# Eight staging buffers for values, key matrix products through six more banks, and eight token statistics ahead of the loop, in a fused cross-attention and expert layer

## The chip, the cores and the metric

The kernel runs on one core of one Trainium2 chip. The metric is device time in microseconds of one execution, the median of the runs taken; lower is better. TensorE (PE), VectorE (DVE), ScalarE (ACT), GpSimd (POOL) and SyncE (SP, which issues most of the DMAs) each work off a list of their own in order and wait for each other by semaphores.

## What is computed

`x` is 4 x 1024 x 256, the context 4 x 77 x 256. A cross-attention of 16 heads is added to `x`, then a layer of 9 experts, of which each token takes two:

```python
x = x + xattn(ctx, layernorm(x), fside)     # the tokens ask, the context answers
x = x + ffn(layernorm(x))

# xattn: kv = layernorm(ctx) @ Wkv; q = (layernorm(x) @ Wq) * (1 + scale) + shift
#        out = softmax(q k^T / 8) v, all heads, @ Wout
# ffn:   w, idx = top_k(softmax(x @ Wr), 2), w normalised to sum 1
#        out[t] = sum over the two experts of w * ((silu(x[t] @ Wg[e]) * (x[t] @ Wu[e])) @ Wd[e])
```

## The kernel before

All products are made in single-precision pieces: each operand is split into a rounded high part, which ScalarE writes, and the rest, which VectorE makes by subtraction; TensorE multiplies hi by hi, hi by lo and lo by hi.

The work has three stages. **Preparation** (to about 54 us) folds the weights into the context. A *key matrix* `keymat` holds Wq times the keys of each head, so that a token's scores are one product of its normalised row; a *value matrix* holds the values times Wout. **Attention** goes over 32 blocks of 128 tokens in steps: scores, softmax, product with the value matrix, routing, scatter of the rows to their experts. **Experts** goes over 40 tiles of rows (32 of 256 rows, 8 of 128) with weights that are loaded, split and multiplied.

The change touches the end of the preparation and the first two steps of attention.

*Key products.* The loop over `m` in 0 to 15 (`MATS`, PE from L1505) makes `keymat`: two matmuls for odd `m` (L1523), four for even `m` (L1523 and L1527), into a pair of PSUM banks that `mat_banks(m)` names. ScalarE copies the pair to `keymat_hi` (L1150, semaphore `mat_hi`), then VectorE subtracts to make `keymat_lo` (`mat_rest`, L1832, `mat_lo`); only then is the pair of banks free. Before the change the pairs are 4-5 and 6-7 in turn, with 2-3 for product 14, so that product `m` waits for the subtraction of product `m - 2`. Ahead of product 14 TensorE turns the first token block (`turn`, L1501, bank 5).

*Values.* Behind each of the first eight key products come two value products (`val`, L1489, two pairs of the banks 0 to 3), 16 in all. ScalarE (12 of them, L1133) and VectorE (4 of them, L1852) copy each to a staging buffer `val_st` in SBUF. Two products fill a buffer of four heads; SyncE stores a full one to DRAM in 4 or 6 DMAs (`store_vals`, L635), 8 buffers' worth in 40 DMAs. With `STORE_BUFFERS` of 4, filling 4 to 7 first waits for the store of the buffer four earlier (`val_stored`). Behind the 40, SyncE waits for them all to land (L641) and loads the value matrix back in the layout that attention wants (`load_valmat`, L651). The 8 late value products are made in the first two attention steps; VectorE copies them (L1852) into `late_f` and `valmat_f`, which lie over the memory of `val_st`, so each of those copies waits for all early stores: a wait on each of the `val_stored` semaphores (L1849).

*Token statistics.* VectorE takes batch statistics of the tokens (`token_stats`, L1838), two blocks behind each of the first seven key subtractions, blocks 0 to 13. GpSimd makes scale and offset from the first eight, and ScalarE normalises the first token block with them behind its copy of product 11.

*The first two token steps.* VectorE's order in step 0 is: minimum over the scores of bank 0, late copy 16, minimum of bank 1 (L1915), late copy 17, logits (L1924), minimum of bank 2, lower half of the next turned token (`zn_rest`, L1858), late copies 18 and 19. TensorE's scores of the second block (L360 to L362) wait for that `zn_rest`.

Of the kernel before, what the change touches and what calls it, by code (L numbers as in the profile page):

```python
# [20 lines left out]
F32 = mybir.dt.float32  # L21
# [8 lines left out]
P = 128  # L30
# [6 lines left out]
TB = S // P  # L37
# [7 lines left out]
BM = B * M  # L45
# [10 lines left out]
X_PARTS = [(0, TB), (TB, TB + 6), (TB + 6, 2 * TB), (2 * TB, 3 * TB), (3 * TB, T)]  # L56
WQ_PARTS = [(0, PAIRS // 2), (PAIRS // 2, PAIRS)]
MAT_VALS = 2
ROUTER_AT, ROUTER_REST_AT, NORM_AT = 8, 10, 11
STATS_DONE = 4  # L60
VALS_FROM = 4
STORE_HEADS = 4
STORE_BUFFERS = 4
LATE_VALS = 4
IDLE = (30, 32, 4)
POOL_GAPS = 2
# [63 lines left out]
def program(nc, x, ctx_rows, fside, ln1_w, ln1_b, ln2, wq, wkv, wout, wr, wg, wu, wd, wout_turned, wr_top, out):  # L130
# [3 lines left out]
    with ExitStack() as ctx:  # L134
        def sem(name):
            return ctx.enter_context(nc.semaphore(name))

        def sb(name, shape, dt=F32, on=ctx):
            return on.enter_context(nc.sbuf_tensor(name, shape, dt))

        banks = ctx.enter_context(nc.psum_tensor("banks", [P, 8, 512], F32))
# [121 lines left out]
        early.close()  # L263
        val_st = [sb(f"val_st{i}", [P, STORE_HEADS, DE], F32, prep) for i in range(STORE_BUFFERS)]
        prep.close()
# [15 lines left out]
        ffn = ExitStack()  # L281
# [12 lines left out]
        tok_gate = sb("tok_gate", [P, NOTES, WB], F32, ffn)  # L294
        tok_id = sb("tok_id", [P, NOTES, WB], I32, ffn)
        wgt = sb("wgt", [P, WEIGHT_SLOTS, WCOLS], F32, ffn)
        wgt_hi.append(sb("wgt_hi1", [P, WCOLS], F32R, ffn))
        tables = ExitStack()
        count = sb("count", [P, E], F32, tables)
# [110 lines left out]
        val_moved = [sem(f"val_moved{i}") for i in range(2)]  # L410
        mat_made = sem("mat_made")
        mat_hi = sem("mat_hi")
        mat_lo = sem("mat_lo")
        val_stored = [sem(f"val_stored{i}") for i in range(STORE_BUFFERS)]
        valmat_loaded = sem("valmat_loaded")
# [84 lines left out]
        SOON_VALS = SOON_STORES * STORE_PAIRS  # L500
        MATS = PAIRS * KT
        TURN_AT = MATS - 2
# [21 lines left out]
            return bank[n % 4 if n < 4 else (n - 4) % 3]  # L524

        def mat_banks(m):
            first = 2 if m == TURN_AT else 4 + 2 * (m % 2)
            return banks[:, first:first + 2, 0:BM]

        def mat_source(m):  # L530
            return mat_banks(m).rearrange("p i (b k) -> p i b k", b=B)
# [15 lines left out]
        def store_place(n):  # L547

            return (n // (CR - 1), n % (CR - 1)) if n < SOON_STORES else (n - SOON_STORES, CR - 1)

        def staging(n):
            return val_st[n % STORE_BUFFERS] if n < SOON_STORES else late_st[n - SOON_STORES]

        def stored_before(n):

            return sum(16 * len(BATCH_PARTS[store_place(i)[1]]) for i in range(n % STORE_BUFFERS, n, STORE_BUFFERS))

# [3 lines left out]
        def key_place(m):  # L561

            return m // KT, m % KT
# [37 lines left out]
        def _(sp):  # L601
# [25 lines left out]
            def store_vals(n):  # L627

                group, r = store_place(n)
                heads = slice(group * STORE_HEADS, (group + 1) * STORE_HEADS)  # L630
                for moved in val_moved:
                    sp.wait_ge(moved, n + 1)
                for r0, r1, b in BATCH_PARTS[r]:
                    k = r * P + r0 - b * M
                    sp.dma_start(valmat_dram[b, heads, k:k + r1 - r0, :].rearrange("h k n -> k h n"),  # L635
                                 staging(n)[r0:r1]).then_inc(val_stored[n % STORE_BUFFERS], 16)

            for n in range(SOON_STORES):
                store_vals(n)
            for n in range(SOON_STORES, SOON_STORES + STORE_BUFFERS):  # L640
                sp.wait_ge(val_stored[n % STORE_BUFFERS], stored_before(n))  # L641
# [166 lines left out]
        def _(pool):  # L808
# [65 lines left out]
            def x_variance(b):  # L874

                own = slice(b * TB, (b + 1) * TB)
                done = b * X_CHAIN
                mean, odd, var = (z[:, own] for z in (x_mean, x_odd, x_var))
                pool.wait_ge(x_counted, b + 1)
                nc.gpsimd.tensor_tensor(odd, x_stats[:, own, 4], x_stats[:, own, 1], ALU.subtract).then_inc(x_chain, 1)  # L880
                nc.gpsimd.tensor_tensor(var, x_stats[:, own, 2], x_stats[:, own, 5], ALU.add).then_inc(x_chain, 1)
                nc.gpsimd.tensor_tensor(mean, x_stats[:, own, 1], x_stats[:, own, 4], ALU.add).then_inc(x_chain, 1)
                pool.wait_ge(x_chain, done + 2)
                nc.gpsimd.tensor_tensor(odd, odd, odd, ALU.mult).then_inc(x_chain, 1)
                nc.gpsimd.tensor_scalar(var, var, 4.0 / D, None, ALU.mult).then_inc(x_chain, 1)
                pool.wait_ge(x_chain, done + 5)
                nc.gpsimd.tensor_tensor(var, var, odd, ALU.add).then_inc(x_chain, 1)
# [94 lines left out]
            def step(s, c):  # L982
# [14 lines left out]
                if ahead < B:  # L997
                    if s % TB == STATS_DONE - 1:
                        x_variance(ahead)
                    elif s % TB == STATS_DONE:  # L1000
                        x_root(ahead, 0)
                    elif s % TB == STATS_DONE + 1:
                        x_root(ahead, 1)
                    elif s % TB == STATS_DONE + 2:
                        x_offset(ahead)
# [365 lines left out]
        def _(pe):  # L1371
# [122 lines left out]
            def turn(s, c):  # L1494

                if c >= 0:
                    pe.wait_ge(turn_moved, s + 1)
                    pe.wait_ge(zn_split, s + 1)
                pe.wait_ge(zn_ready, s + 2)
                for k in range(KT):  # L1500
                    mm = nc.tensor.transpose(bank[5][:, k * P:(k + 1) * P], zn[(c + 1) % 2][:, k * P:(k + 1) * P], ident[:])  # L1501
                mm.then_inc(turn_done, 1)


            for m in range(MATS):  # L1505
                c, k = key_place(m)
                if m < 2:
                    pe.wait_ge(keys_moved, PAIRS - 2 + 2 * m)
                if c == WQ_PARTS[0][0]:
                    pe.wait_ge(heads_made, 1)  # L1510
                elif c == WQ_PARTS[1][0]:
                    pe.wait_ge(pool_heads_made, 2)
                if m == TURN_AT:
                    pe.wait_ge(mat_lo, TURN_AT - 1)
                    turn(-1, -1)
                    for moved in val_moved:
                        pe.wait_ge(moved, SOON_VALS // 2)
                if m >= 2:
                    pe.wait_ge(mat_lo, m - 1)
                to = mat_banks(m)  # L1520
                halves = [slice(i * DH, (i + 1) * DH) for i in range(2)]
                for i, half in enumerate(halves):
                    mm = nc.tensor.matmul(to[:, i, :], wq_sb[half, c, k * P:(k + 1) * P], k_scale[half, c, :],  # L1523
                                          start=True, stop=k > 0)
                if not k:
                    for i, half in enumerate(halves):
                        mm = nc.tensor.matmul(to[:, i, :], to_first[half, :], k_shift[half, c, :], start=False, stop=True)  # L1527
                mm.then_inc(mat_made, 1)
                if m < SOON_VALS // MAT_VALS:
                    val(2 * m)  # L1530
                    val(2 * m + 1)
# [232 lines left out]
        def _(dve):  # L1764
# [70 lines left out]
            def token_stats(t0, t1):  # L1835
                for t in range(t0, t1):
                    dve.wait_ge(x_loaded[next(i for i, part in enumerate(X_PARTS) if t < part[1])], 16)
                    ins = nc.vector.bn_stats(x_stats[:, t, :], xs[:, t * D:(t + 1) * D])  # L1838
                if t1 % TB == 0:
                    ins.then_inc(x_counted, 1)  # L1840
# [13 lines left out]
            def zn_rest(s, c):  # L1854
# [3 lines left out]
                nc.vector.tensor_tensor(to[1][:], bank[5][:, 0:KT * P].rearrange("p (k n) -> p k n", n=P), to[0][:].bitcast(F32),  # L1858
                                        ALU.subtract).then_inc(zn_split, 1)

            for m in range(MATS):
                if m == ROUTER_REST_AT:
                    dve.wait_ge(wr_cols_hi, 1)
                    for k in range(KT):
                        hi, lo = (z[:, :, k * HKE + HK:(k + 1) * HKE] for z in keymat)
                        ins = nc.vector.tensor_tensor(lo, wr_dev[:, k, :].unsqueeze(1).to_broadcast([P, B, EX]), hi.bitcast(F32),
                                                      ALU.subtract)
                    ins.then_inc(wr_cols_split, 1)
                if m == TURN_AT:
                    zn_rest(-1, -1)  # L1870
                mat_rest(m)
                if m < SOON_VALS // MAT_VALS:
                    if m % 2:
                        val_move(2 * m + 1)
                    if 2 * m < X_PARTS[1][1]:
                        token_stats(2 * m, 2 * m + 2)

            def val_rest(b, g):

# [101 lines left out]
            def step(s, c):  # L1981
# [47 lines left out]
                if ahead < B:  # L2029
                    t = ahead * TB + 2 * (s % TB)  # L2030
                    if s % TB < STATS_DONE and t >= X_PARTS[1][1]:
                        token_stats(t, t + 2)
# [335 lines left out]
```

## Time and profile before

| what | us |
|---|---|
| median of the runs | 805.01 (lowest 804.41) |
| profiled execution | 803.48 |
| its span, from first to last instruction | 801.3 |
| TensorE busy in the span | 771.7 (96%) |
| VectorE busy | 649.0 (81%) |
| ScalarE busy | 609.9 (76%) |
| GpSimd busy | 387.4 (48%) |

One of the three runs took 1660.45 us, and the median leaves it aside. TensorE's clock was granted in full (0.993 of 2.4 GHz on the mean). Busy shares are means over the three stages; what the change is worth has to be read where it acts, in the first 70 us.

### The profile page before, as it was taken

Reading aid. Unit: us, or ns where it says so; the run is one execution under the profiler, and the core shown is the slowest. Engines: PE = TensorE matmul, PEld = TensorE weight load, DVE = VectorE, ACT = ScalarE, POOL = GpSimd, SP = SyncE. Lnnn points to the kernel's source line nnn. Section 1 sums busy time; section 2 is a strip of 40 time slices with the busy share of each in tenths; the row PEclk is TensorE's granted clock in tenths of the full one; section 3 lists DMA queues with packets and bytes.
Section 4 is the critical chain, followed back from the end, with each engine's and each line's share of the span. In section 5 each row is a group of like instructions: output and inputs, shape, how many; then the busy total and the mean of one; then the engine's idle time right before and its main releaser. Section 6 shows DMA issues by size and latency. Waiting matters only on the chain.

```text
span 801.3 us, 19758 instructions
## 1 busy us (share of the span) xinstructions
PE 771.7 (96%) x6057; PEld 738.6 (92%) x6057; DVE 649.0 (81%) x1584; ACT 609.9 (76%) x1942; POOL 387.4 (48%) x541
## 2 busy tenths in 40 slices
PE   9978999999999999997999999999999999999994
PEld 8747999999999999897999999999999999999994
DVE  6667888888888878887778888787897888879782
ACT  4759998898889888734777778787777877778762
POOL 5602687787688667762332243333333333233343
PEclk9999999999999999999999999999999999999998
DMA  8576401400401111645574463565666656473322
GB/s 309 162 199 187 136 28 35 152 28 34 152 28 34 61 55 41 205 133 152 143 214 106 105 174 80 124 148 146 165 153 165 152 144 169 104 205 81 49 24 28
DMA packets 78211, 96.39 MB, mean 120 GB/s; under 512 B 10851, under 2 KB 65307, under 8 KB 77979
## 3 DMA queue, kind: packets, MB, share of 16 engines
q1 hardware_dynamic: 64667, 77.25, 31.3%
q0 software_dynamic: 13440, 17.90, 12.7%
q8 instruction: 48, 0.79, 0.4%
q14 instruction: 56, 0.46, 0.2%
HBM read 109.46 MB, written 30.23 MB: 174 GB/s over the span
## 4 chain that ended last, share of the span: by engine, by line
PE 82%; DVE 5%; POOL 4%; ACT 3%; issue 2%; DVEq 1%; DMA 1%; SPq 1%; POOLq 0%; ACTq 0%
PE banks L360 23%; PE banks L361 23%; PE banks L362 23%; PE banks L1548 3%; PE banks L1714 2%; PE banks L1405 2%; PE banks L1562 2%; DVEq L1767 1%; ACT prob L1165 1%; POOL prob L979 1%; POOL expert_in L950 1%; PE banks L1501 1%; PE banks L1489 1%; PE banks L1523 1%; POOL result L1041 1%
## 5 line engine op out<-in xcount | busy, mean ns | idle before, releaser
L360 PE MATMUL banks<-tok_t_hi,wgt_hi 128*128 128x256 f32 x704 | 201.3, 286 | 4.2 <-issue 3.0
L1041 POOL DMA_INDIRECT result<-res,tok_id x72 | 121.4, 1687 | 165.6 <-ACT res L1300 145.9
L362 PE MATMUL banks<-tok_t_hi,wgt_lo 128*128 128x256 f32 x704 | 196.9, 280 | 0.0
L361 PE MATMUL banks<-tok_t_lo,wgt_hi 128*128 128x256 f32 x704 | 196.8, 279 | 0.0
L1165 ACT ACTIVATE prob<-banks,row_min 128x77 f32<-128x77 f32 x512 | 161.6, 372 | 2.3 <-DVE row_min L1915 2.3
L360 PEld LDWEIGHTS banks<-tok_t_hi,wgt_hi 128*128 128x128 f32 x704 | 133.6, 190 | 6.2 <-issue 6.1
L361 PEld LDWEIGHTS banks<-tok_t_lo,wgt_hi 128*128 128x128 f32 x704 | 133.1, 189 | 0.0
L362 PEld LDWEIGHTS banks<-tok_t_hi,wgt_lo 128*128 128x128 f32 x704 | 132.9, 189 | 0.0
L1165 ACT ACTIVATION_READ_ACCUMULATOR prob<-banks,row_min 128x1 f32 x512 | 129.3, 254 | 0.0
L360 PE MATMUL banks<-wgt_hi,hid_hi 128*128 128x256 f32 x360 | 100.9, 280 | 0.7 <-DVE hid_hi L2231 0.7
L361 PE MATMUL banks<-wgt_lo,hid_hi 128*128 128x256 f32 x360 | 100.5, 279 | 0.0
L362 PE MATMUL banks<-wgt_hi,hid_lo 128*128 128x256 f32 x360 | 100.0, 278 | 0.0
L979 POOL TENSOR_TENSOR prob<-prob,row_inv 128x1232 f32<-128x1232 f32 x32 | 72.1, 2254 | 55.0 <-DVE row_inv L1929 55.0
L2186 DVE TENSOR_TENSOR wgt_lo<-wgt,wgt_hi 128x704 fp32r<-128x704 f32 x116 | 97.8, 883 | 0.5
L360 PE MATMUL banks<-valmat_hi,prob_t_hi 128*128 128x266 f32 x320 | 94.6, 295 | 0.5 <-DVE logits L1937 0.5
L361 PE MATMUL banks<-valmat_lo,prob_t_hi 128*128 128x266 f32 x320 | 91.6, 286 | 0.0
L362 PE MATMUL banks<-valmat_hi,prob_t_lo 128*128 128x266 f32 x320 | 91.4, 286 | 0.0
L1235 ACT ACTIVATE wgt_hi<-wgt 128x704 fp32r (+1 forms) x116 | 85.0, 785 | 3.4 <-DMA wgt<-in_L_ffn_Wu 3.4
L950 POOL DMA_INDIRECT expert_in<-xn,top_slot x64 | 66.2, 1035 | 38.6 <-POOL xn L936 25.9
L1012 POOL COPY tok_gate<-tok 128x2 f32<-128x2 f32 (+1 forms) x40 | 21.5, 538 | 121.3 <-DMA result<-res,tok_id 121.3
L360 PE MATMUL banks<-keymat_hi,zn_t_hi 128*128 128x462 f32 (+1 forms) x192 | 72.8, 379 | 0.6 <-ACT prob L1165 0.5
L1180 ACT ACTIVATE prob_t_hi<-banks 128x512 fp32r<-128x512 f32 (+1 forms) x96 | 48.7, 542 | 30.9 <-PE banks L1548 30.9
(280 smaller groups left out, 2173.0 us busy)
## 6 DMA issues: line engine op xcount, KB each, us to landing
wgt<-in_L_ffn_Wg SPq DMA_DIRECT2D x29, 704.0 KB
wgt<-in_L_ffn_Wu SPq DMA_DIRECT2D x29, 640.0 KB
wgt<-in_L_ffn_Wd SPq DMA_DIRECT2D x29, 640.0 KB
tok<-expert_in SPq DMA_DIRECT2D x32, 258.0 KB, 3.7
spare_wgt<-in_L_ffn_Wg SPq DMA_DIRECT2D x9, 704.0 KB, 4.3
spare_wgt<-in_L_ffn_Wu SPq DMA_DIRECT2D x9, 640.0 KB, 6.2
spare_wgt<-in_L_ffn_Wd SPq DMA_DIRECT2D x9, 640.0 KB, 6.3
valmat_f<-valmat_dram SPq DMA_DIRECT2D x4, 1197.0 KB, 6.2
```

The costliest lines, as they stand in the source:

```text
L360: nc.tensor.matmul(to, a[0], b[0], start=first, stop=False)
L361: nc.tensor.matmul(to, a[0], b[1], start=False, stop=False)
L362: return nc.tensor.matmul(to, a[1], b[0], start=False, stop=last)
L950: nc.gpsimd.indirect_dma_start(expert_in, bass.IndirectOffsetOnAxis(ap=top_slot[c % 4][:, k:k + 1], axis=0), xn[c % 4][:, k, :], None).the ...
L979: nc.gpsimd.tensor_tensor(p, p, row_inv[i][:].unsqueeze(2).to_broadcast([P, H, M]), ALU.mult).then_inc(prob_ready, 1)
L1012: nc.gpsimd.tensor_copy(tok_gate[:, t % NOTES, 0:blocks], tok[i][:, 0:blocks, GATE])
L1041: nc.gpsimd.indirect_dma_start(out, bass.IndirectOffsetOnAxis(ap=tok_id[:, t % NOTES, a:a + 1], axis=0), res[i][:, a, :], None, compute_op ...
L1165: ins = nc.scalar.activation(prob[c % 2][:, h * M:(h + 1) * M], bank[i][:, (h - h0) * M:(h - h0 + 1) * M], ACT.Exp, bias=row_min[c % 2][:, ...
L1180: ins = nc.scalar.activation(prob_t[c % 2][0][0:rows, m0:m1, :], turned_bank(c, g, rows, m0 - c0, m1 - c0), ACT.Copy)
L1235: nc.scalar.activation(wgt_hi[half_of(t)][:, p0:p1], src[:, p0:p1], ACT.Copy).then_inc(weights_hi, 1)
L1548: mm = nc.tensor.transpose(bank[3 + (c * NG + g) % 2][0:n, (m - c0) * P:(m - c0 + 1) * P], prob[c % 2][:, m * P:m * P + n], ident[:])
L2186: nc.vector.tensor_tensor(wgt_lo[i][:, p0:p1], src[:, p0:p1], wgt_hi[i][:, p0:p1].bitcast(F32), ALU.subtract).then_inc(weights_split, 1)
```

## The change

Four edits. The value products get eight staging buffers, one for each early store. The key products from 10 on go through banks that the value products have left: a table names the first bank of each product's pair, product `m` waits for the last product that had the same pair (`mats_before`), and the first use of banks 0 to 3 (products 10 and 11) waits for the value copies instead. The statistics of the first eight token blocks stand ahead of the loop of key subtractions, and only blocks 8 to 13 stay inside it. In the experts' memory, 128 bytes of nothing are put behind the loaded weights `wgt`, which moves `wgt_hi1` and `wgt_lo1`, the split weights of every second tile, by as much.

```diff
+MAT_BANKS = (4, 6, 4, 6, 4, 6, 4, 6, 4, 6, 0, 2, 6, 0, 2, 6)
-STORE_BUFFERS = 4
+STORE_BUFFERS = 8
...
         wgt = sb("wgt", [P, WEIGHT_SLOTS, WCOLS], F32, ffn)
+        sb("line_gap2", [P, 32], F32, ffn)
         wgt_hi.append(sb("wgt_hi1", [P, WCOLS], F32R, ffn))
...
         def mat_banks(m):
-            first = 2 if m == TURN_AT else 4 + 2 * (m % 2)
-            return banks[:, first:first + 2, 0:BM]
+            return banks[:, MAT_BANKS[m]:MAT_BANKS[m] + 2, 0:BM]
+        def mats_before(m):
+            return max(n for n in range(m) if MAT_BANKS[n] == MAT_BANKS[m]) + 1
...
                 if m == TURN_AT:
-                    pe.wait_ge(mat_lo, TURN_AT - 1)
+                    pe.wait_ge(mat_lo, MAT_BANKS.index(0) - 1)
                     turn(-1, -1)
-                    for moved in val_moved:
-                        pe.wait_ge(moved, SOON_VALS // 2)
                 if m >= 2:
-                    pe.wait_ge(mat_lo, m - 1)
+                    if MAT_BANKS[m] >= 4 or MAT_BANKS[m] in MAT_BANKS[:m]:
+                        pe.wait_ge(mat_lo, mats_before(m))
+                    else:
+                        for moved in val_moved:
+                            pe.wait_ge(moved, SOON_VALS // 2)
...
+            token_stats(0, TB)
             for m in range(MATS):
...
-                    if 2 * m < X_PARTS[1][1]:
-                        token_stats(2 * m, 2 * m + 2)
+                    if TB + 2 * m < X_PARTS[1][1]:
+                        token_stats(TB + 2 * m, TB + 2 * m + 2)
```

TensorE keeps its order of instructions; its waits change. Key products 10 to 13 before (each `banks<-k_scale,wq_sb` row with a wait opens a product):

```order
L1523 MATMUL banks<-k_scale,wq_sb 128x308 [waits mat_lo]
L1523 MATMUL banks<-k_scale,wq_sb 128x308
L1527 MATMUL banks<-k_shift,to_first 128x308 x2
L1523 MATMUL banks<-k_scale,wq_sb 128x308 [waits mat_lo]
L1523 MATMUL banks<-k_scale,wq_sb 128x308
L1523 MATMUL banks<-k_scale,wq_sb 128x308 [waits mat_lo]
```

And now, where products 10 and 11 wait for the value copies:

```order
L1530 MATMUL banks<-k_scale,wq_sb 128x308 [waits val_moved1,val_moved0]
L1530 MATMUL banks<-k_scale,wq_sb 128x308
L1534 MATMUL banks<-k_shift,to_first 128x308 x2
L1530 MATMUL banks<-k_scale,wq_sb 128x308 [waits val_moved1,val_moved0]
L1530 MATMUL banks<-k_scale,wq_sb 128x308
L1530 MATMUL banks<-k_scale,wq_sb 128x308 [waits mat_lo]
```

No row has moved; the `mat_lo` that is left asks for the product three or four back.

On VectorE the start of the key loop before (`x_stats` are the token statistics, `val_st` the staging buffers):

```order
L1832 TENSOR_TENSOR keymat_lo<-banks,keymat_hi 128x2x4x77
L1838 BN_STATS x_stats<-xs 128x6 x2
L1832 TENSOR_TENSOR keymat_lo<-banks,keymat_hi 128x2x4x77
L1852 COPY val_st<-banks 128x532
L1838 BN_STATS x_stats<-xs 128x6 x2
```

And now:

```order
L1845 BN_STATS x_stats<-xs 128x6 x8
L1839 TENSOR_TENSOR keymat_lo<-banks,keymat_hi 128x2x4x77
L1845 BN_STATS x_stats<-xs 128x6 x2
L1839 TENSOR_TENSOR keymat_lo<-banks,keymat_hi 128x2x4x77
L1859 COPY val_st<-banks 128x532
```

Eight statistics now stand ahead of the first subtraction.

## Rows read from the trace of the kernel before

**Rows 1.** Windows: stretch, its length, busy us of each engine, PE clock, DMA.
```profile
core 0: us, PE busy (x) PEld busy (x) DVE busy (x) ACT busy (x) POOL busy (x), PEclk, DMA share, GB/s
28.00:40.00 12.00, 12.00 (x98) 8.20 (x94) 10.77 (x22) 9.03 (x16) 4.60 (x12) 1.00 0.59 143
40.00:54.00 14.00, 9.21 (x64) 5.48 (x61) 7.81 (x15) 7.88 (x16) 1.47 (x6) 1.00 0.74 192
142.00:206.00 64.00, 64.00 (x471) 61.26 (x469) 56.72 (x207) 56.63 (x291) 49.15 (x83) 1.00 0.21 67
```

**Rows 2.** Timeline of TensorE: start, duration, instruction, idle time ahead and its releaser.
```profile
41.16 1.22 PE L1489 MATMUL banks<-xs 64*128 64x266 f32 x8 [0.89 <-ACT val_st L1133]
42.22 0.69 PE L1523 MATMUL banks<-k_scale,wq_sb 64*128 64x308 f32 x4
...
43.26 0.71 PE L1523 MATMUL banks<-k_scale,wq_sb 64*128 64x308 f32 x4
45.64 0.79 PE L1523 MATMUL banks<-k_scale,wq_sb 64*128 64x308 f32 x4 [1.68 <-DVE keymat_lo L1832]
...
53.63 0.48 PE L360 MATMUL banks<-keymat_hi,zn_t_hi 128*128 128x462 f32 x1
...
60.27 0.47 PE L360 MATMUL banks<-keymat_hi,zn_t_hi 128*128 128x462 f32 x1
```

**Rows 3.** Timeline of ScalarE.
```profile
40.50 1.12 ACT L1133 ACTIVATE val_st<-banks 128x532 f32<-128x532 f32 x2 [1.01 <-DMA valmat_dram<-val_st]
41.50 0.69 ACT L1150 ACTIVATE keymat_hi<-banks 128x616 fp32r<-128x616 f32 x1
43.56 0.61 ACT L1133 ACTIVATE val_st<-banks 128x532 f32<-128x532 f32 x1 [1.37 <-DMA valmat_dram<-val_st]
...
67.48 2.71 ACT L1173 ACTIVATE valmat_hi<-valmat_f 128x798 fp32r<-128x798 f32 x4
```

**Rows 4.** Timeline of VectorE.
```profile
28.87 0.80 DVE L1832 TENSOR_TENSOR keymat_lo<-banks,keymat_hi 128x616 fp32r<-128x616 f32 x1 [5.43 <-ACT keymat_hi L1150]
29.59 0.74 DVE L1838 BATCH_NORM_STATS2 x_stats<-xs 128x6 f32<-128x256 f32 x2
...
47.72 1.51 DVE L1832 TENSOR_TENSOR keymat_lo<-banks,keymat_hi 128x616 fp32r<-128x616 f32 x2 [1.09 <-ACT keymat_hi L1150]
...
56.22 0.70 DVE L1852 COPY late_f<-banks 52x532 f32<-52x532 f32 x1 [0.20 <-PE banks L1489]
58.11 0.64 DVE L1915 TENSOR_REDUCE row_min<-banks 128x6 f32<-128x462 f32 x1 [1.19 <-PE banks L362]
...
59.80 0.41 DVE L1858 TENSOR_TENSOR zn_t_lo<-banks,zn_t_hi 128x256 fp32r<-128x256 f32 x1
```

**Rows 5.** Timeline of SyncE's DMA issues; duration from first to last of a group.
```profile
8.08 10.29 SPq L622 DMA_DIRECT2D xs<-in_x  x2
29.93 22.77 SPq L635 DMA_DIRECT2D valmat_dram<-val_st  x40
54.45 0.38 SPq L651 DMA_DIRECT2D valmat_f<-valmat_dram  x1
```

**Rows 6.** Waits of SyncE, 0 to 80 us: total, times, longest.
```profile
SPq L641 <- DMA valmat_dram<-val_st: 1.6, 1, 1.6
```

**Rows 7.** DMA, 0 to 80 us: 40 slices of 2 us; issues, KB, us to landing.
```profile
GB/s 7 171 233 388 397 387 406 398 357 349 350 343 63 8 4 68 215 209 136 224 205 154 211 214 166 208 183 28 315 313 111 104 11 111 119 19 313 375 339 347
...
valmat_f<-valmat_dram SPq DMA_DIRECT2D x2, 1197.0 KB, 5.9
```

**Rows 8.** DMA issues from 8 to 13 us.
```profile
xs<-in_x SPq DMA_DIRECT2D x1, 1024.0 KB, 16.1
```

**Rows 9.** VectorE's sequencer at the line of the late copies' store waits: durations in ns.
```profile
L1849 DVEq EVENT_SEMAPHORE  x16: 49/50/50, 55.2 to 66.2; - x16
```

**Rows 10.** Windows of TensorE alone, two stretches of 48 gate and up products.
```profile
446.11:451.55 5.44, 5.44 (x50) 1.00 0.04 2
489.56:495.22 5.66, 5.66 (x50) 1.00 0.16 13
```

**Rows 11.** Timeline of GpSimd.
```profile
24.51 2.37 POOL L857 TENSOR_TENSOR wq_sb<-wq_sb,ln_rows 128x1024 f32<-128x1024 f32 x1
```

## Prediction

> **What bounds the kernel now.** I read the sum by stage first, then one engine after another through the 40 us that the change touches, then the DMA queue beside them. By stage [rows 1], TensorE is busy for all of 28 to 40 us (products that make the key matrix, four value products behind each) and for all of 142 to 206 us (attention steps), but for only 9.21 of the 14 us from 40 to 54. That hole is what the change is about.
>
> The rows of TensorE [rows 2] name it. At 41.16 it waited 0.89 us until ScalarE had emptied a value bank, and at 45.64 it waited 1.68 us until VectorE had finished the key product two before. The second wait has two shorter ones like it further on, because the last key products go round on two pairs of banks: one must be rounded by ScalarE and subtracted by VectorE before the second next may start. ScalarE [rows 3] shows why the first wait is there: at 40.50 and at 43.56 it stood 1.01 and 1.37 us for a store of an older staging buffer to land. Then I looked at who feeds the next stage: SyncE's queue issues the 40 stores of the staged values from 29.93 on for 22.77 us with little pause, waits 1.6 us for the last to land [rows 6], and at 54.45 issues the load behind them [rows 5].
>
> **The change, part by part.** The sum is made against the profiled execution, 803.48 us (span 801.3 and 2.2 around it); the median of the runs shown is 805.01, 1.5 above it, and I carry that over.
>
> *Eight staging buffers.* Stores 4 to 7 no longer wait for stores 0 to 3, so the waits at 40.50 and 43.56 go [rows 3], and TensorE's value products of 41.16 start at 40.27, 0.89 earlier [rows 2].
>
> *Six more banks.* From product 10 on, three to four products are in flight. What is left per two products is TensorE's own 1.56 us (an even one 1.04, from 42.22 to 43.26 [rows 2], an odd one half of it) and VectorE's 1.51 us (the pair at 47.72 [rows 4]); ScalarE needs less (two of 0.69 that overlap [rows 3]). Step by step: values 40.27 to 41.33, product 8 to 42.37, product 9 to 42.89, product 10 then at once (its banks were emptied by VectorE about 42.5). It stood at 45.64, so this is 2.75 earlier. From product 10 to the first scores it took 53.63 - 45.64 = 7.99 us; now 3 x 1.56 = 4.7, one wait of 0.6 for product 9's subtraction, the 0.4 of the turn and 0.3 for its second half: 6.0. The first scores start about 48.9 instead of 53.63, 4.7 earlier [rows 2].
>
> *Where that stall goes.* I do not think that the 4.7 us survive. The late values go into buffers that share memory with the staging buffers, so VectorE's first late copy, at 56.22 before [rows 4], waits until all 40 early stores have landed. Before, the stores were through at 54.4 [rows 5, 6], and VectorE came 1.8 us later: no wait. Now it would come near 51.4 and stand there until 54.4. More buffers do not help the queue: it waits for values only at its start, and the first seven products, which feed it, stay on TensorE's pace [rows 1]. Behind the copy VectorE's queue is held: the second row minimum, a copy, the logits, the third minimum and the lower half of the next turned token. These ran from 58.11 to 59.80 + 0.41 = 60.21 without a gap, 2.10 us [rows 4]. New: copy 54.45, 0.61 later (0.70 less the overlap that such pairs show) the minimum at 55.06, end of the block 57.16; TensorE starts the second token's scores 0.06 later, at 57.22 instead of 60.27 [rows 2]. **That is 3.05 us earlier.** The ScalarE stretch behind it follows: its valmat rounding at 67.48 [rows 3] moves to 64.4, and what it reads was issued at 54.45 [rows 5] and landed 5.9 us later [rows 7], about 60.4, so it is still in time by 4 us. From there on each step follows the one before at TensorE's pace [rows 1] and the shift is carried to the end.
>
> *Eight statistics ahead of the loop.* VectorE stood still for 5.43 us before the first keymat subtraction at 28.87; two statistics take 0.74, 0.66 net of overlap [rows 4], so eight take 2.64. Their token part was issued at 8.08 [rows 5] and landed 16.1 later [rows 8], at 24.2: done at 26.9, 2.0 us before they are missed. That also takes work out of products 3 to 6, but TensorE sets the pace there. Nothing, while the load is in time.
>
> *More semaphores.* Each late copy now waits for eight store semaphores in place of four. The wait instruction takes 50 ns and there are 16 for eight copies [rows 9]: two more each, 0.1 us on VectorE's sequencer, ahead of time while the engine is at work. Between 0 and 0.2 us on the path; I take 0.
>
> *Second weight slot 128 bytes on.* No row shows a shifted tile. TensorE has two paces in the last stage: the stretch of 48 products took 5.44 us in one tile and 5.66 in another, of the same length and with no wait in either [rows 10]; both occur in odd and in even tiles, so the slot does not pick it. There are about 26 such stretches, half at either pace. If the address were to turn all of the odd ones to one pace, that would be some 6 or 7 stretches x 0.22, and as much again in the down products: 3 us either way. I take 0 and keep both ends.
>
> Sum: 803.5 - 3.05 = 800.4 on the profile's scale, **801.9 us** on that of the median.
>
> **A place where a rule can be weighed.** In the new place the eight statistics run from 24.2 to 26.9 beside GpSimd's multiply at 24.51, which took 2.37 us with VectorE idle [rows 11] and which ScalarE's first keymat instruction (about 28.2, ahead of the subtraction at 28.87 [rows 4]) waits for. No row shows this pair side by side, so by rows alone GpSimd may lose nothing, or all of 2.64 us. The Trainium skill ("SBUF — State Buffer", section "Who interferes with whom") says that a VectorE instruction with at most one SBUF input, outside the two-port modes, does not contend with GpSimd; a batch statistic has one. By the rule the sum stays at 3.05; no run here shows it yet.
>
> **Rivals.**
> 1. *The stores are not the bound*, because the queue goes faster with its buffers free: the whole 4.7 us stays, 798.8 + 1.5 = 800.3. For it: nothing in the trace; against it, 40 issues in 22.77 us, 0.57 each, with no sign that the queue waited for a buffer [rows 5].
> 2. *GpSimd loses to the statistics*: its multiply ends at 29.5 instead of 26.9, the first keymat instruction comes 1.4 us late, and with it values and stores. 3.05 - 1.4 = 1.65: 803.4. The row for its length when alone [rows 11] says nothing on it.
> 3. *The shift is absorbed later*, at a transfer or a table that does not move: 805.0, no change. Against it: in 142 to 206 us TensorE never stops [rows 1].
> 4. *The weight slot decides the pace*, 3 us to either side of the forecast: 798.9 or 804.9.
> 5. *Slower: the token load is late.* The statistics are now at the head of VectorE's queue and all of the keymat loop is behind them. If the load lands after 26.2, each us costs one; from 29.3 on the change loses. If the 16.1 us counted from the end of its issue (the issues of both token parts take 10.29 us together [rows 5], half of it ends at 13.2) instead of the start, it would land at 29.3, the statistics end at 32.0, and VectorE start its loop 3.1 us late: 805.0; a load of a us more, 806. Against it: in slices of 2 us the DMA rate falls from 343 to 63 and 8 GB/s after 24 us [rows 7], so the loads were through by 26.
>
> **How the numbers follow.** Forecast 0.64, rival 1 0.08, rival 2 0.09, rival 3 0.05, rival 4 0.05 on either side, rival 5 0.04. The point is the forecast's, 801.9. Its own range, by the pace lottery (26 stretches x 0.2 at random, about 1 us) and the 0.6 between the runs shown, is 800.4 to 803.3. Up to 804.2 and down to 799.8 takes in rivals 1 and 2 and leaves out 3, 5 and both halves of 4, 0.19 in all. Faster or slower by over 2% means 16 us, about what a measurement of this kernel can tell from no change; no case reaches it: 0.01 faster, 0.98 within, 0.01 slower.
>
> **What would show it.** Right: no idle time of ScalarE ahead of a value copy; the waits of TensorE between products 10 and 15 gone but for one of about 0.6; first scores near 48.9; VectorE's first late copy idle for about 3 us behind "DMA valmat_dram<-val_st" and starting near 54.45; second scores near 57.2. Wrong: a late copy near 51.5 (rival 1), a GpSimd multiply of over 4 us (rival 2), a first keymat subtraction after 29 us (rivals 2 and 5), or attention steps whose start has moved by 3 us and an end that has not (rival 3, 4).

## The result, and the profile after

| | kernel before | changed kernel |
|---|---|---|
| median, us (range of the runs) | 804.53 (803.03 to 805.01) | 798.34 (797.59 to 800.57) |
| ratio, 95% interval | | 0.9934 [0.9916, 0.9951] |
| profiled execution, us | 803.48 | 799.43 |
| its span | 801.3 | 797.6 |
| TensorE / VectorE / ScalarE busy | 771.7 / 649.0 / 609.9 | 769.0 / 649.1 / 609.9 |

By the ratio the time is 5.3 us (3.9 to 6.8) less, 0.7%; the two medians lie 6.2 us apart. Forecast were 3.05 us and 801.9; the time came out below the range. One execution of before took 1660.45 us and is left out of the range and the ratio.

TensorE's timeline in the changed kernel answers to [rows 2] (start, duration, instruction, idle time ahead and what ended it):

```profile
40.11 1.17 PE L1494 MATMUL banks<-xs 64*128 64x266 f32 x8
...
44.76 0.79 PE L1530 MATMUL banks<-k_scale,wq_sb 64*128 64x308 f32 x4 [0.25 <-DVE keymat_lo L1839]
...
48.73 0.48 PE L362 MATMUL banks<-keymat_hi,zn_t_hi 128*128 128x462 f32 x1
...
53.81 0.38 PE L1506 MATMUL banks<-ident,zn 128*128 128x128 f32 x2
55.94 0.66 PE L1494 MATMUL banks<-xs 64*52 64x266 f32 x4 [1.75 <-DVE late_f L1859]
57.10 0.66 PE L1494 MATMUL banks<-xs 64*52 64x266 f32 x4 [0.51 <-DVE late_f L1859]
57.95 0.48 PE L362 MATMUL banks<-keymat_hi,zn_t_hi 128*128 128x462 f32 x1 [0.19 <-DVE zn_t_lo L1865]
```

The hole from 40 to 54 us is gone and the first scores are 4.9 us earlier. At 55.94 there is a new one. VectorE, SyncE and ScalarE of the changed kernel show why, and what it leaves:

```profile
24.31 2.71 DVE L1845 BATCH_NORM_STATS2 x_stats<-xs 128x6 f32<-128x256 f32 x8 [0.86 <-DMA xs<-in_x]
28.88 0.80 DVE L1839 TENSOR_TENSOR keymat_lo<-banks,keymat_hi 128x616 fp32r<-128x616 f32 x1 [1.86 <-ACT keymat_hi L1155]
...
55.18 0.70 DVE L1859 COPY late_f<-banks 52x532 f32<-52x532 f32 x1 [4.15 <-DMA valmat_dram<-val_st]
```

```profile
29.94 23.43 SPq L640 DMA_DIRECT2D valmat_dram<-val_st  x40
55.16 0.39 SPq L656 DMA_DIRECT2D valmat_f<-valmat_dram  x1
```

```profile
39.40 1.11 ACT L1138 ACTIVATE val_st<-banks 128x532 f32<-128x532 f32 x2
40.94 0.65 ACT L1138 ACTIVATE val_st<-banks 128x532 f32<-128x532 f32 x1
...
65.17 2.71 ACT L1178 ACTIVATE valmat_hi<-valmat_f 128x798 fp32r<-128x798 f32 x4
```

VectorE stands 4.15 us for the stores to land. ScalarE no longer waits ahead of a value copy [rows 3]. The second scores are 2.32 us earlier than in [rows 2] and the valmat rounding (ScalarE's copy of the value matrix to `valmat_hi`) 2.31 earlier than in [rows 3], so of the 3.7 us of span 1.4 come later on. Where, show VectorE's rows of the first single tile (a tile of 128 rows) and of the last tile, before:

```profile
418.45 0.42 DVE L2215 TENSOR_TENSOR single_hid<-single_act,banks 128x256 f32<-128x256 f32 x1 [1.43 <-ACT single_act L1272]
...
786.66 0.42 DVE L2205 TENSOR_TENSOR hid_f<-gate_act,banks 128x256 f32<-128x256 f32 x1 [1.65 <-ACT gate_act L1268]
```

and after:

```profile
416.09 0.42 DVE L2223 TENSOR_TENSOR single_hid<-single_act,banks 128x256 f32<-128x256 f32 x1 [1.58 <-ACT single_act L1277]
...
783.03 0.42 DVE L2213 TENSOR_TENSOR hid_f<-gate_act,banks 128x256 f32<-128x256 f32 x1 [1.75 <-ACT gate_act L1273]
```

Between them lie 368.21 us before and 366.94 after, 1.27 less, in a stage that the change touches by 128 bytes of address only. I call this length the *last stretch* below.

### The profile page after: what moved, and what is told of

Read it like the earlier page. It is cut to its first block, busy times and chain, and to the rows that moved or that the text cites. A ratio compares the mean times of both kernels' runs of the same rounds, so it can differ in the third digit from the quotient of the medians.

```text
span 797.6 us, 19771 instructions
## 1 busy us (share of the span) xinstructions
PE 769.0 (96%) x6057; PEld 736.7 (92%) x6057; DVE 649.1 (81%) x1584; ACT 609.9 (76%) x1942; POOL 389.4 (49%) x541
## 4 chain that ended last, share of the span: by engine, by line
PE 87%; DVE 4%; POOL 3%; issue 2%; ACT 2%; SPq 1%; DVEq 1%; DMA 1%; POOLq 0%; ACTq 0%
PE banks L362 25%; PE banks L363 24%; PE banks L364 24%; PE banks L1555 4%; PE banks L1721 2%; PE banks L1410 2%; PE banks L1569 2%; SPq L640 1%; PE banks L1494 1%; PE banks L1506 1%; DVEq L1774 1%; POOL expert_in L955 1%; POOL prob L984 1%; PE banks L1530 0%; PE banks L1693 0%
## 5 line engine op out<-in xcount | busy, mean ns | idle before, releaser
L1017 POOL COPY tok_gate<-tok 128x2 f32<-128x2 f32 (+1 forms) x40 | 24.3, 607 | 121.0 <-DMA result<-res,tok_id 120.9
```

The source lines that it names most:

```text
L1017: nc.gpsimd.tensor_copy(tok_gate[:, t % NOTES, 0:blocks], tok[i][:, 0:blocks, GATE])
```

## The experiments

**The 128 bytes alone, and all but them**

```diff
 # 128 bytes alone: into the kernel before; all but them: out of the changed one
+        sb("line_gap2", [P, 32], F32, ffn)
```

> The kernel before with the 128 bytes ahead of the second weight slot alone; nothing else is changed. Theory A (the slot sets TensorE's pace in the last stage): the part of the gain that the first 67 us do not explain is the slot's, 1.4 us by the two profiles (3.7 us of span less 2.3) to 3.0 us by the medians (5.3 less 2.3), so 801.5 to 803.1 beside a kernel before of 804.5; the seven stretches of 37 down products behind the single tiles, 4.63 to 4.66 us each in the kernel before, take 4.50 as in the changed one. Theory B (the pace is chance from one execution to the next): ratio 1.000 within 0.001, and the stretches of 37 are at either length.

A *stretch of 37* is 37 rows of TensorE's timeline: the 34 down products of a tile of 256 rows and behind them three rows of transposes for a single tile, counted from the first start to the last. The expectations call all of it down products.

Measured: 803.67 us, ratio 0.9985 [0.9972, 0.9997], 1.2 us less than before, a little under the 1.4 to 3.0 expected; all stretches of 37 at 4.49 to 4.54 (there are eight of them, not seven); last stretch 367.46.

> The changed kernel without the 128 bytes ahead of the second weight slot; the buffers, the banks and the statistics stay. Theory A: 1.4 to 3.0 us longer than the changed kernel, 799.7 to 801.3, and the stretches of 37 down products are back at 4.64 us. Theory B: as the changed kernel, 798.3 within 1 us, which leaves the gain beyond 2.3 us unexplained by the slot. By both: second scores near 57.9 us and the valmat rounding at 65.2, as in the changed kernel.

Measured: 801.29 us, 0.9956 [0.9939, 0.9972]; seven of the eight stretches of 37 at 4.63 to 4.66, the last one at 4.50; last stretch 369.21; valmat rounding 64.70. Theory A holds in both directions. TensorE from the start of the first stretch of 37 to the first product behind it (windows: length, busy, matmuls, clock), before and after:

```profile
418.86:423.55 4.69, 4.69 (x44) 1.00 1.01 251
```

```profile
416.50:421.02 4.52, 4.52 (x43) 1.00 0.98 249
```

Busy throughout and at full clock in both, and 0.17 us apart. The eight of them, 4.65 against 4.50 on the mean, make 1.2 us. That is not the whole account. Eight times, between a single tile's down products and the next tile, TensorE stands with nothing that the profile shows to wait for (total, times, longest; 418 to 787 us before, 416 to 784 after):

```profile
PE banks L360 <- issue: 2.8, 8, 0.5
```

```profile
PE banks L362 <- issue: 4.1, 8, 0.7
```

So 1.3 us of the faster pace go into longer pauses, and the products themselves gain 2.6 us over the last stretch, in the gate and up products as well as in the down products.

**First late places free of the early buffers**

```diff
-late_st = [x[:, 1, i:i + STORE_HEADS, :] for x in (late_f, valmat_f) for i in (0, STORE_HEADS)]
+late_st = [x[:, 1, i:i + STORE_HEADS, :] for x, i in
+           ((valmat_f, 2), (valmat_f, 2 + STORE_HEADS), (late_f, 0), (late_f, STORE_HEADS))]
...
-                if n >= SOON_STORES:
+                if n >= SOON_STORES + 2:
                     for i in range(SOON_STORES, SOON_STORES + STORE_BUFFERS):
...
-                elif n >= STORE_BUFFERS:
+                elif STORE_BUFFERS <= n < SOON_STORES:
```

> The changed kernel with the first two staging places of the late values put where no early staging buffer lies (the upper end of valmat_f), so that the first four late copies wait for no store; the other two places, in late_f, keep the wait. Theory C (VectorE's first late copy, held until all 40 early stores have landed, is what took back the gain of the banks): the copy starts at 51 to 51.6 us instead of 55.18, the second scores near 54 instead of 57.9, and the valmat rounding comes 3 to 4 us earlier than 65.17, held by its load (issued behind the stores at 55.2, landed some 5.9 us later, 61.1): 794.5 to 795.5. Rival D (the load of the value matrix, which is issued behind the same stores, holds the rounding anyway, or the copies that keep the wait are next to stand in VectorE's queue): the copy is early and the rounding is not, 797.5 to 798.5.

Measured: 797.29 us, 0.9900 [0.9886, 0.9914], 6.9 to 9.2 us less than before and the shortest of all. VectorE and ScalarE of this kernel:

```profile
51.30 0.70 DVE L1859 COPY valmat_f<-banks 52x532 f32<-52x532 f32 x1 [0.20 <-PE banks L1494]
```

```profile
62.59 2.71 ACT L1178 ACTIVATE valmat_hi<-valmat_f 128x798 fp32r<-128x798 f32 x4
```

The copy is early, waits for TensorE instead of the stores, and the rounding comes 2.58 us earlier than in the changed kernel: theory C holds, its gain somewhat under the 3 to 4 us expected. SyncE still needed 23.32 us for its 40 issues.

**The banks alone**

```diff
-STORE_BUFFERS = 8
+STORE_BUFFERS = 4
 # and without line_gap2, with the statistics in the loop as before
```

> The kernel before with the table of banks and its waits alone: four staging buffers, the statistics in the loop, no shift of the slot. Theory C: ScalarE's two waits for stores near 40.5 and 43.5 us stay and the first scores come near 49.6 us, 0.9 later than in the changed kernel, but the late copy stands for the same stores (through at 54.4 to 55.2), so the second scores come near 57.2 to 58 all the same, and with them 2.3 us of gain: 802.2 beside a kernel before of 804.5. Rival E (each part brings its share, and the buffers bring the stores through earlier): 803 or more, with the stores through later than in the changed kernel by the 0.9 us.

Measured: 802.24 us, 0.9965 [0.9952, 0.9978]. First scores at 50.24, 1.5 later than in the changed kernel, yet the late copy still stood, until 54.63:

```profile
54.63 0.70 DVE L1858 COPY late_f<-banks 52x532 f32<-52x532 f32 x1 [2.10 <-DMA valmat_dram<-val_st]
```

The rounding came at 64.62, 2.86 us earlier than before. The banks alone bring all of the gain of this place, as theory C said; the buffers' share goes into the stall.

**Other steps of the slot** (e5: 64 bytes, e6: 256, e10: 384; e7: the bytes ahead of `wgt_lo1` only; e11: ahead of both halves, so that the lower lies 256 on)

```diff
-        sb("line_gap2", [P, 32], F32, ffn)
+        sb("line_gap2", [P, 16], F32, ffn)      # e5; 64 in e6, 96 in e10
...
+        sb("line_gap3", [P, 32], F32, ffn)      # e11; in e7 this one alone
         wgt_lo.append(sb("wgt_lo1", [P, WCOLS], F32R, ffn))
```

> The changed kernel with 64 bytes ahead of the second weight slot instead of 128. The mark is the seven stretches of 37 down products behind the single tiles: 4.63 to 4.66 us each where there are no bytes ahead of the slot, 4.49 to 4.54 with 128. Theory F (any step off the old place does it): 4.50, and the time of the changed kernel. Theory G (the old and the new place lie at either half of a pattern that repeats, and 64 bytes are between): 4.64 or something between the two, and the time of the changed kernel with 1 to 2 us added.

> The changed kernel with 256 bytes ahead of the second weight slot instead of 128. Theory F (any step off the old place does it): stretches of 37 at 4.50 us and the time of the changed kernel. Theory G (a pattern that repeats every 256 bytes): back to 4.64 us, and 1 to 2 us longer than the changed kernel.

> The changed kernel with the 128 bytes ahead of the lower half of the second weight slot (wgt_lo1) alone; the upper half (wgt_hi1) stays where it was in the kernel before, and the lower half lies where it does in the changed kernel. Theory H (the place of the lower half sets the pace): stretches of 37 at 4.50 us and the time of the changed kernel. Theory I (the place of the upper half does): 4.64 us, and 1 to 2 us longer. If each half has its share, between the two, about 4.57.

> The changed kernel with 384 bytes ahead of the second weight slot instead of 128. Theory G (the pattern repeats every 256 bytes; 0 and 256 bytes gave the same lengths): stretches of 37 down products at 4.50 us as with 128, and from the first single tile to the last tile 366.9 to 367.7 us, as with 128, not 368.2 to 369.3, as with 0 and 256; time of the changed kernel. Rival: 4.64 and 368.2 to 369.3, that is, only 128 itself is good.

> The changed kernel with another 128 bytes between the two halves of the second weight slot: the upper half 128 bytes on as in the changed kernel, the lower half 256 bytes on. If the pattern repeats every 256 bytes this shifts the upper half alone. Theory I (the place of the upper half sets the pace; the lower half alone brought nothing): stretches of 37 at 4.50 us and 366.9 to 367.7 us from the first single tile to the last. Rival (both halves must move together): 4.64 us and 368.2 or more, up to 2 us longer than the changed kernel.

Measured, with the kernels that have the slot in the same place:

| bytes ahead of upper / lower half | kernel: ratio to before | stretches of 37, us | last stretch, us |
|---|---|---|---|
| 0 / 0 | before; e2 0.9956 [0.9939, 0.9972] | 4.63 to 4.66 (one of e2's at 4.50) | 368.21; 369.21 (e4 369.26, e13 368.89) |
| 256 / 256 | e6 0.9972 [0.9961, 0.9983] | 4.63 to 4.66 | 368.76 |
| 128 / 128 | changed 0.9934; again (e12) 0.9943 | 4.49 to 4.53 | 366.94; 367.26 (five others up to 367.67) |
| 384 / 384 | e10 0.9936 [0.9923, 0.9949] | 4.49 to 4.50 | 367.10 |
| 64 / 64 | e5 0.9999 [0.9989, 1.0009] | half 4.49, half 4.67 | 370.76 |
| 0 / 128 | e7 0.9963 [0.9950, 0.9976] | 4.63 | 369.02 |
| 128 / 256 | e11 0.9974 [0.9964, 0.9983] | 4.50 and 4.70 | 369.30 |

Theory G holds: 256 bytes are as none, 384 as 128. (The bytes ahead of both halves also shift small routing tables that share the memory of `wgt_lo1`; their last use, at 369.5 us before, lies ahead of the last stretch.) F falls, and so do H and I, since either half moved alone brings nothing in sum. It isn't without effect: in e11 the stretches of 48 gate and up products are shorter than in any other kernel (the 28 behind 380 us, from the first start to the next product's, add up to 154.9 us, 156.0 in the changed kernel), and the down products longer. With 64 bytes other stretches lengthen too (the stretches of 48 reach 5.71, where the longest of before is 5.62). The means are 368.9 us with 0 or 256 bytes (five kernels, 368.2 to 369.3) and 367.3 with 128 or 384 (eight, 366.9 to 367.7): the slot is worth 1.6 us. The pauses go with the place too: 2.8 to 3.1 us with 0 or 256 bytes, 3.9 to 4.2 with 128 or 384, so that the pace alone is worth some 2.7 us. Which access of the weights meets which other access there stays open; the traces show only the lengths, and not why the pauses grow.

**Four buffers, once the late places are free**

```diff
-STORE_BUFFERS = 8
+STORE_BUFFERS = 4
```

> The kernel with the first two late staging places free of the early buffers (797.3 us, first scores 48.81, valmat rounding 62.59), with four staging buffers instead of eight. Theory J (the eight buffers bring their 0.9 to 1.4 us once the late copy no longer stands for the stores; with the banks alone the first scores came at 50.24): ScalarE's two waits for stores are back, first scores near 50.2, the valmat rounding near 64.0, 798.2 to 798.8. Rival K (the buffers bring nothing, another wait takes over): 62.6 and 797.3.

Measured: 798.46 us, 0.9921 [0.9906, 0.9936]; ScalarE's waits are back (1.09 and 0.80 us), first scores at 50.03, rounding at 63.79. Theory J: the eight buffers are worth 1.2 us at the rounding, but only where nothing stands for the stores.

**The hole made longer, and the changed kernel again**

```diff
                         dve.wait_ge(val_stored[i % STORE_BUFFERS], stored_before(i))
+                    if m == SOON_VALS:
+                        nc.vector.memset(staging(n + 1), 0.0)
```

> The changed kernel with one memset of 1064 columns, about 1.1 us, on VectorE between the wait for the stores and the first late copy: the hole in TensorE's work that ends at 55.94 us is longer by that much. Theory M (a hole of TensorE is paid twice once it is long enough, since the granted clock falls behind it: in two profiles of kernels with this hole, those with 64 bytes and with the lower half alone, it fell to 0.5 to 0.6 in 57 to 60 us and the valmat rounding came 1.3 us late, 66.1 to 66.5, and in three others it did not, 64.7 to 65.2): the clock falls here, the copy starts at 56.3, and the valmat rounding comes 2.3 to 2.4 us later than 65.17, near 67.5; time 2.3 us over the changed kernel. Rival N (the fall is chance and has nothing to do with the hole's length): granted clock 1.00, rounding 1.1 us later, near 66.3, and 1.1 us over the changed kernel.

> The changed kernel once more beside the others, to size its gain on the same chip. By the parts measured so far it is 2.3 to 3.3 us from the first 330 us (banks alone 2.8, all but the slot 3.5 by the medians; 2.3 to 2.9 by the profiles at the valmat rounding) and 1.2 to 1.5 us from the slot: 3.5 to 4.8 us less than before, ratio 0.9940 to 0.9956. If the first measurement (0.9934) is right in its middle, 5.3 us, and 0.5 to 1.8 us are of neither part.

Measured: e9 802.21 us, 0.9975 [0.9965, 0.9985]; the changed kernel again 800.12 us, 0.9943 [0.9930, 0.9956], 4.6 us (3.5 to 5.6) less than before. The windows behind the hole (length, busy us of PE, PEld, DVE, ACT, POOL, granted clock, DMA) of the changed kernel's first profile, of its second, and of e9:

```profile
54.00:57.00 3.00, 0.85 (x6) 0.17 (x4) 1.82 (x4) 0.92 (x5) 0.00 (x0) 1.00 0.32 60
57.00:60.00 3.00, 2.71 (x16) 1.64 (x18) 2.47 (x8) 3.00 (x19) 0.00 (x1) 1.00 1.03 343
```

```profile
54.00:57.00 3.00, 1.19 (x9) 0.35 (x8) 2.42 (x6) 1.52 (x9) 0.00 (x0) 1.00 0.41 93
57.00:60.00 3.00, 2.81 (x10) 1.87 (x8) 1.79 (x4) 2.52 (x15) 0.59 (x1) 0.55 1.08 365
```

```profile
57.00:60.00 3.00, 2.30 (x12) 1.24 (x9) 2.95 (x7) 2.72 (x19) 0.00 (x0) 0.83 1.08 366
60.00:63.00 3.00, 3.00 (x13) 1.44 (x12) 1.52 (x3) 1.97 (x12) 2.18 (x1) 0.60 0.66 182
```

The late copy and the rounding of the second profile:

```profile
54.58 0.70 DVE L1859 COPY late_f<-banks 52x532 f32<-52x532 f32 x1 [3.68 <-DMA valmat_dram<-val_st]
```

```profile
66.08 2.71 ACT L1178 ACTIVATE valmat_hi<-valmat_f 128x798 fp32r<-128x798 f32 x4
```

The same kernel kept the granted clock at 1.00 behind the hole in one execution and went down to the lower of the two levels (1.2 of 2.4 GHz) for most of 57 to 60 us in the other. There the rounding came at 66.08 although the late copy, at 54.58, was 0.60 earlier than in the first profile: the fall costs 0.91 + 0.60 = 1.5 us. Of nine profiles with this hole (changed kernel twice, e2, e5, e6, e7, e10, e11, e14) four show the fall (e5, e7, e11, e12). From the late copy to the rounding it takes 9.98 to 9.99 us in the five without it and 11.23 to 11.57 in the four with it, 1.2 to 1.6 us more. Of the five kernels in which nothing stands for the stores (before, e1, e3, e8, e13) none shows a fall at this place, nor does e4, where VectorE stands but TensorE pauses there for no more than 0.28 us at a time.

In e9 the clock fell and the rounding was at 67.57, as theory M said, and its median lies 2.1 us over that of the changed kernel, not 1.1. But a fall occurs without the longer hole too, and among the nine the length doesn't sort them: TensorE's wait for the late copy was 1.29 to 1.74 us in the four with a fall and 1.30 to 1.82 in the five without. So one profile doesn't show that the length decides it. That the clock falls because of the hole fits four falls of nine with it and none of six without; it isn't shown.

**The statistics alone, and all but them**

```diff
+            token_stats(0, TB)
             for m in range(MATS):
...
-                    if 2 * m < X_PARTS[1][1]:
-                        token_stats(2 * m, 2 * m + 2)
+                    if TB + 2 * m < X_PARTS[1][1]:
+                        token_stats(TB + 2 * m, TB + 2 * m + 2)
```

> The kernel before with the eight statistics ahead of VectorE's loop alone. Theory P (the order of the statistics brings the 0.47 us outside the span, and nothing within it): time less span 1.85 instead of 2.33 us, valmat rounding near 67.5 as before, 0.5 us less than before (ratio 0.9994, which is about the width of a measurement). Rival Q (it is the sum of the changes or the length of the program, not this step): 2.33, and the time of the kernel before.

> The changed kernel with the statistics in the loop as before; the buffers, the banks and the 128 bytes stay. Theory P: time less span back at 2.33 us, the first keymat subtraction at 28.9 and the second scores at 57 to 58 us as in the changed kernel, 0.5 us over it (799.5 to 800.6 beside 804.4). Rival R (the statistics in the loop hold VectorE in products 3 to 6): first scores later than 48.8, more than 0.5 us over the changed kernel.

Measured: alone 804.78 us, 0.9999 [0.9989, 1.0008], time less span 2.37 us (median of the runs, as in what follows); taken out again 800.41 us, 0.9946 [0.9931, 0.9961] beside 0.9943 with them, time less span 1.84. So the statistics bring nothing that these runs can tell, and theory P falls: they don't bring the 0.47 us outside the span (time less span: some 2.33 us before, 1.86 after) either. The kernel before has 2.26 to 2.37 us there in the series beside these runs, those with one of the four edits (e1, e4, e13) 2.30 to 2.37, all with several 1.83 to 1.88. What the last share is not found; e8, with four buffers, has 1.86, so it isn't the eight buffers, which were not run alone.

In both of these profiles the granted clock fell in another place: 0.54 in 27 to 30 us of e13, whose rounding came at 68.78, 1.30 us later than in [rows 3], and 0.50 there in e14. So the first scores of e14, at 50.09, don't weigh rival R, which wants them later than 48.8 and over 0.5 us more; a difference of that size lies within the two intervals, so R stays open.

## Why the forecast missed

*Eight buffers, six banks: right.* Values at 40.11 (forecast 40.27), first scores at 48.73 (48.9), one wait of 0.25 us left in between (0.6). E4 and e8 add that the buffers do nothing while the stall behind them stands, and 1.2 us once it is gone.

*Where the stall goes: right in mechanism, near in size.* It reappeared at the first late copy, behind the store landing. E3 and E4 show it: without that dependence the copy comes at 51.30, and with the banks alone it stands until the same landing. From the copy to the second scores it took 2.77 us, exactly the forecast's 57.22 - 54.45. The copy came at 55.18, not 54.45, since the 40 issues took 23.43 us, not the 22.77 of [rows 5] that I carried over; in the other kernels with this stall they took 22.89 to 23.35 and the copy came at 54.58 to 55.19 (e9, with its memset, and e14, late throughout, aside). Part of that goes with the buffers: 22.77 to 22.98 us in the five kernels with four of them, 23.06 to 23.43 in the eleven with eight. At the rounding that left 2.31 us in the first profile and 2.6 to 2.9 in e2, e4, e6 and e10, against 3.05. What I did not see: the stall is also a hole in TensorE's work, and in some executions the clock falls behind it, at 1.2 to 1.6 us.

*Statistics and semaphores: right, nothing.* The loop starts at 28.88 after 28.87 [rows 4]; GpSimd's multiply took 2.37 us beside the eight statistics, as alone [rows 11]. Rivals 2 and 5 fall.

```profile
24.58 2.37 POOL L862 TENSOR_TENSOR wq_sb<-wq_sb,ln_rows 128x1024 f32<-128x1024 f32 x1
```

By the rule of the Trainium skill ("SBUF — State Buffer", section "Who interferes with whom") this pair does not contend; the trace agrees, 2.37 us in both.

*Second weight slot: the step that failed.* I took 0 because both paces occur in odd and in even tiles, "so the slot does not pick it". The stretch that I judged by, 48 products [rows 10], does mix, with more lengths than the two that I read. The stretch of 37 does not: before, all eight took 4.63 to 4.66 us, and with the slot 128 bytes on all take 4.49 to 4.53. One kind of stretch was read for all of them. Measured, the step brings 1.6 us; rival 4 was right in kind and had too small a chance. Its price of 3 us is near the 2.7 that the pace gains; the longer pauses behind the single tiles, which no term had, take 1.2 of it back. The 64 bytes of e5 show the other end: a loss of the same order, 1.9 us in the last stretch.

*Rivals 1 and 3.* Rival 1 falls: with eight buffers the stores are no faster. Rival 3 falls: the 2.3 us at 65 us were 2.9 early in the expert stage (347.05 after 349.93).

*The sum, and the second step that failed.* Put together as measured: 2.3 to 2.9 us at the rounding, 1.6 for the slot and 0.47 outside the span make 4.4 to 5.0, against 5.3 (3.9 to 6.8) and 4.6 (3.5 to 5.6) measured. On the profile's own scale the forecast was 800.4 and the profiled execution took 799.43, 1.0 us less: 1.3 for the slot and 0.35 outside the span in these two profiles, less the 0.7 by which the stall was mis-sized, come to most of it. Even with the slot's 1.6 us in it the forecast would have been 800.3, 2.0 above the measured median. The larger part of the miss in the median, 2.6 of 3.6 us, is the step from there to the median, "I carry that over": I added the 1.5 us by which the profile of before lay under its median, and that of after lay 1.1 over its own.

The two series of the same changed kernel have medians of 798.34 and 800.12; the 1.8 us between them are not assigned. Falls of the clock would fit: in the second series the three longest executions, 800.12 to 800.93, had a mean granted clock of 0.989, the two shortest, 798.91 and 799.04, 0.991 and 0.992. Where the clock fell is known only for the profiled one, so that is not shown.

## What to carry to other kernels

When a stall is taken out, ask what the released engine will wait for next, and look for a place where that dependence is only one of memory: here free space for two buffers (e3) was worth nearly as much again as the banks. Don't judge an address change by one kind of stretch: sort the stretches by what they multiply, look for a kind that always has the longer of two lengths, and add up the pauses between them as well. A single profiled execution places the steps well, but its distance to the median is no constant to carry over where a few us matter.

## What the runs showed of the hardware

- Moving both halves of a weight buffer by 128 bytes changes the length of busy TensorE stretches by 3% (4.64 to 4.50 us). 256 bytes act as none and 384 as 128; 64 bytes make the last stretch 1.9 us longer, and one half moved alone brings nothing in sum. The pauses of TensorE behind the single tiles go the other way (2.8 to 3.1 us in all with 0 or 256 bytes, 3.9 to 4.2 with 128 or 384), and nothing in the profile says what ends them.
- Behind a hole of TensorE of some 2 us (1.3 to 1.8 in its longest wait) the granted clock fell to its lower level in four of nine profiles, at 1.2 to 1.6 us each; the same kernel shows it in one execution and not in another. Behind the longer hole near 366 us, where TensorE waits for the experts' first rows (`tok<-expert_in`, 2.91 us before), it falls in each of the profiles, and for different lengths.
- 40 store issues on SyncE's queue take 22.77 to 22.98 us with four buffers behind them and 23.06 to 23.43 with eight: free buffers did not speed them up.
- 0.47 us of the gain lie outside the span. The slot, the banks and the statistics alone don't bring them; the eight buffers alone were not run, and a kernel without them has them too.
